# Turning z of the first two tiles and u of the last on TensorE instead of by transposing transfers

## The chip, the cores and the metric

The kernel runs on one core of a Trainium2 chip. The metric is the device time of one execution in microseconds; the median of three runs is used. The profile is of one further execution.

## What is computed

```python
# x: (64, 64, 512) fp32; cond: (64,) int32; w_cond: (200, 64, 64)
# w_up: (1024, 512); w_down: (512, 1024)
def hbitlinear(x, w, bits):
    xq = act_quant(fwht(x), bits)      # per token: scale = 127 / max|x|, round, clip, divide
    wq = weight_quant(w)               # ternary, scale = mean|w|
    return einsum('bsd,fd->bsf', xq, wq)

y = einsum('bct,bcd->bdt', x, w_cond[cond])
h = square(relu(hbitlinear(y, w_up, 8)))
out = x + hbitlinear(h, w_down, 8)
```

fwht is the normalized Walsh-Hadamard transform along the last axis (512 elements for y, 1024 for h).

## The kernel before, in words

The 4096 tokens are worked off in 16 tiles of 256 tokens (t = 0 to 15), each made of two pairs of batch entries (k = 0, 1) with 128 tokens each. For each tile the stages are:

- load_x and gather_w (SP's DMA queue): x and the gathered w_cond blocks, the latter into a block-diagonal w_diag.
- x_outer on POOL (x_first on VectorE for tile 0): the outermost butterfly of the first Hadamard transform.
- project(t, h) on TensorE, h = 0, 1: the projection with w_diag into y_ps[h]. y_split (ACT) copies one half out, and y_outer (VectorE) does a further butterfly into y.
- had_z(t, k) on TensorE: the last 128-wide part of the transform, into one PSUM bank (z_ps; for k = 1 of the tiles under EARLY = 4 it is o_ps).
- z_absmax, z_floor, z_invert on VectorE, and quant_z on ACT: z quantized to fp16 integers in zq, with tokens on partitions.
- turn_z(t): one transposing transfer on ACT's DMA queue, zq to zqT, both halves at once.
- up(t, u) on TensorE, u = 0 to 3, into two PSUM buffers h_ps; relu and square on ACT into g.
- g_outer and g_inner on VectorE and g_last on POOL: three butterflies of the second transform. The last tile has half-width forms of these (g_outer_last, g_inner_last, g_last_last).
- had_u(t, k) on TensorE into u_ps (k = 0 of the last two tiles: the banks of h_ps); u_absmax, u_floor, u_invert on VectorE; quant_u on ACT into uq.
- turn_u(t, k): a transposing transfer, uq to uqT, again on ACT's queue.
- down(t, k) on TensorE: eight accumulating matmuls; the residual on VectorE adds x, and SP stores. Tile 14 goes to the banks of y_ps, tile 15 to o_ps and z_ps.

keep_z, token_units and u_unscale on POOL carry the scales along. At the start both weights are loaded in four parts each, summed (weight_abs on ACT and VectorE, weight_sum on TensorE, weight_scale on VectorE), rounded (weight_round, ACT), turned by TensorE (weight_turn, eight transposes into half of u_ps) and evicted (weight_evac, VectorE). warm(i) is four matmuls on constants, which fill TensorE's idle time at the start.

Every engine has its own order of stages, written out by hand: begin() for the pipeline's filling, a step() that the loop repeats for steps 8 to 15, with a fixed lag for every stage, and finish() for its emptying. Semaphores are all that ties the engines together. An engine that waits holds everything behind it in its order. TensorE's finish() ends with:

```python
at(had_u, 15, 0)
at(had_u, 15, 1)
at(down, 14, 1)
at(down, 14, 0)
at(down, 15, 0)
at(down, 15, 1)
```

Of the kernel before, what the change touches and what calls it, by code (L numbers as in the profile page):

```python
# [61 lines left out]
EARLY = 4  # L62
LAST = TILES - 1
# [3 lines left out]
def ffn_kernel(nc, x, cond, w_cond, w_up, w_down, had, out):  # L67
# [7 lines left out]
    with ctx:  # L75
# [102 lines left out]
        s_zqT = sem("zqT_ready")  # L178
        s_kept = sem("z_kept_ready")
# [82 lines left out]
        def _(sp):  # L262
# [43 lines left out]
            at(gather_w, 0, 0)  # L306
            at(load_x, 1, 0)
            at(load_x, 1, 1)
            at(gather_w, 1, 0)
            at(gather_w, 1, 1)  # L310
            load_w_down(3)
            load_w_down(1)
            at(gather_w, 2, 0)
            at(load_x, 2, 0)
            at(load_x, 2, 1)
            at(gather_w, 2, 1)
            load_w_down(0)
            load_w_down(2)
            at(load_x, 3, 0)
            at(gather_w, 3, 0)  # L320
            at(load_x, 3, 1)
            at(gather_w, 3, 1)
            at(load_x, 4, 0)
            at(load_x, 4, 1)
            at(gather_w, 4, 0)
            at(gather_w, 4, 1)
            at(load_x, 5, 0)
            at(gather_w, 5, 0)
# [5 lines left out]
            at(load_x, 7, 0)  # L334
            at(gather_w, 6, 1)
            at(gather_w, 7, 0)
            at(load_x, 7, 1)
            at(load_x, 8, 0)
            at(store, 0, 0)
            at(gather_w, 7, 1)  # L340
            at(store, 1, 0)
            at(store, 0, 1)
            at(gather_w, 8, 0)
            at(load_x, 8, 1)
            at(gather_w, 8, 1)
            at(load_x, 9, 0)
            at(load_x, 9, 1)
            at(store, 2, 0)
            at(store, 1, 1)
            at(gather_w, 9, 0)  # L350
            at(gather_w, 9, 1)
            at(load_x, 10, 0)
            at(store, 2, 1)
            at(store, 3, 0)
            at(gather_w, 10, 0)
            at(gather_w, 10, 1)
            at(load_x, 10, 1)
            at(load_x, 11, 0)
            at(load_x, 11, 1)
            at(store, 3, 1)  # L360
            at(gather_w, 11, 0)
            at(load_x, 12, 0)
            at(store, 4, 1)
            at(load_x, 12, 1)
            at(load_x, 13, 0)
            at(store, 4, 0)
            at(gather_w, 11, 1)
            at(gather_w, 12, 0)
            at(gather_w, 12, 1)
            hold(1)  # L370
            at(store, 5, 0)
            at(gather_w, 13, 0)
            at(load_x, 13, 1)
            at(store, 5, 1)
            at(load_x, 14, 0)
            at(load_x, 14, 1)
            at(load_x, 15, 0)
            at(store, 6, 0)
            at(gather_w, 13, 1)
            at(store, 7, 0)  # L380
            at(store, 6, 1)
            at(store, 7, 1)
            at(load_x, 15, 1)
            at(gather_w, 14, 0)
            at(gather_w, 14, 1)
            at(store, 8, 1)
            at(store, 8, 0)
            at(gather_w, 15, 0)
# [4 lines left out]
            at(store, 10, 0)  # L393
            at(store, 11, 1)
            at(store, 11, 0)
            at(store, 12, 1)
            at(store, 12, 0)
# [10 lines left out]
        def _(pool):  # L408
# [72 lines left out]
            def begin():  # L481
# [4 lines left out]
                at(x_outer, 2, 0)  # L486
                at(x_outer, 3, 0)
                at(x_outer, 3, 1)
                at(keep_z, 1)
                at(x_outer, 4, 1)  # L490
                at(x_outer, 4, 0)
                at(token_units, 0)
# [9 lines left out]
                at(x_outer, 6, 1)  # L502
                at(x_outer, 6, 0)
                at(u_unscale, 0, 1)
                at(token_units, 1)
                at(keep_z, 4)
                at(g_last, 2, 0)
                at(g_last, 2, 1)
                at(u_unscale, 1, 0)
                at(keep_z, 5)  # L510
                at(u_unscale, 1, 1)
                at(x_outer, 7, 0)
                at(token_units, 2)
                at(x_outer, 7, 1)
                at(g_last, 3, 0)
                at(g_last, 3, 1)
                at(u_unscale, 2, 0)
# [12 lines left out]
            def finish():  # L530
                at(token_units, 11)
                at(keep_z, 14)
                at(g_last, 12, 0)
                at(g_last, 12, 1)
                at(u_unscale, 11, 1)
                at(u_unscale, 11, 0)
# [3 lines left out]
                at(g_last, 13, 1)  # L540
                at(u_unscale, 12, 1)
                at(u_unscale, 12, 0)
# [6 lines left out]
                g_last_last(0, 0)  # L549
                at(u_unscale, 14, 0)  # L550
                g_last_last(1, 0)
                at(u_unscale, 14, 1)
                at(token_units, 15)
                at(u_unscale, 15, 1)
                at(u_unscale, 15, 0)
# [4 lines left out]
        def _(act):  # L560
# [81 lines left out]

            def load_had():
                act.dma_start(had_sb[:, :], had[:, 0, 0:P]).then_inc(s_had, 16)

            def begin():
                load_had()
                load_w_up(1)
                gather_first(0)
                gather_first(1)  # L650
                load_w_up(0)
                load_w_up(2)
                at(y_split, 0, 1)
                at(y_split, 0, 0)
                weight_abs(0, 0)
                load_w_up(3)
                weight_abs(0, 2)
                at(y_split, 1, 1)
                at(quant_z, 0, 0)
                at(y_split, 1, 0)  # L660
                at(quant_z, 0, 1)
                weight_round(0, 0)
                weight_round(0, 1)
                at(turn_z, 0)
                weight_round(0, 2)
                weight_round(0, 3)
                weight_abs(1, 1)
                weight_abs(1, 3)
                at(relu, 0, 1)
                at(relu, 0, 0)  # L670
                at(quant_z, 1, 1)
                at(y_split, 2, 1)
                at(y_split, 2, 0)
                at(square, 0, 0)
                at(quant_z, 1, 0)
                weight_round(1, 0)
                at(y_split, 3, 0)
                weight_round(1, 1)
                at(relu, 0, 2)
                at(turn_z, 1)  # L680
                at(relu, 0, 3)
                at(square, 0, 1)
                at(y_split, 3, 1)
                weight_round(1, 2)
                at(relu, 1, 0)
                at(relu, 1, 1)
                weight_round(1, 3)
                at(quant_z, 2, 0)
                at(y_split, 4, 0)
                at(quant_z, 2, 1)  # L690
                at(relu, 1, 3)
                at(y_split, 4, 1)
                at(relu, 1, 2)
# [3 lines left out]
                at(square, 1, 0)  # L697
                at(relu, 2, 1)
                at(quant_u, 0, 0)
                at(quant_z, 3, 1)  # L700
                at(relu, 2, 0)
                at(relu, 2, 3)
                at(turn_u, 0, 0)
                at(square, 2, 0)
                at(relu, 2, 2)
                at(y_split, 5, 1)
                at(turn_z, 3)
                at(y_split, 5, 0)
                at(quant_z, 4, 0)
                at(quant_u, 0, 1)  # L710
                at(square, 2, 1)
                at(quant_z, 4, 1)
                at(relu, 3, 0)
                at(relu, 3, 1)
                at(turn_z, 4)
                at(y_split, 6, 0)
                at(quant_u, 1, 0)
                at(quant_z, 5, 0)
                at(relu, 3, 3)
                at(turn_u, 0, 1)  # L720
                at(relu, 3, 2)
                at(y_split, 6, 1)
                at(square, 3, 0)
                at(quant_z, 5, 1)
                at(quant_u, 1, 1)
                at(square, 3, 1)
                at(turn_u, 1, 0)
                at(relu, 4, 1)
                at(turn_u, 1, 1)
                at(relu, 4, 0)  # L730
                at(relu, 4, 3)
                at(turn_z, 5)
                at(quant_u, 2, 0)
                at(relu, 4, 2)
                at(quant_z, 6, 0)
                at(y_split, 7, 0)
                at(quant_u, 2, 1)
                at(square, 4, 1)
                at(y_split, 7, 1)
                at(turn_u, 2, 0)  # L740
# [690 lines left out]
```

## Time and profile before

| | |
|---|---|
| median of 3 runs | 264.64 us (263.68 to 269.92) |
| the profiled execution's own time | 267.76 us |
| its span, first to last instruction | 266.0 us |
| TensorE busy | 247.5 us, 93% |
| VectorE busy | 210.4 us, 79% |
| POOL busy | 192.3 us, 72% |
| ACT busy | 146.4 us, 55% |
| TensorE's mean granted clock | 0.992 of full speed |

Busy times are of one execution, and engines work side by side. PE is TensorE, DVE VectorE, ACT ScalarE, POOL GpSimd and SP SyncE; "ACTq" and "SPq" are DMAs as issued by these engines. L879 is a line of the kernel: L837 warm, L847 project, L864 had_z, L827 weight_turn, L879 up, L900 had_u, L917 down on TensorE; L598 quant_z, L634 quant_u, L608 turn_z, L641 turn_u on ACT; L1060 weight_abs, L1092 weight_evac, L1106 y_outer, L1111 z_absmax, L1136 g_inner, L1168 u_absmax, L1187 residual on VectorE; L461 g_last on POOL; L282 gather_w and L292 load_w_down on SP. An fp32 matmul shows up as two passes.

### The profile page before, as it was taken

How to read it: one execution, taken by the hardware profiler on the slowest of the kernel's cores; microseconds unless marked ns; L12 is line 12 of the kernel's file. 1: busy time of each engine (PE TensorE's matmuls, PEld its weight loads, DVE VectorE, ACT ScalarE, POOL GpSimd, SP SyncE). 2: the span in 40 equal slices, each digit the busy share in tenths (PEclk: the TensorE clock that was granted, in tenths of full speed). 3: DMA queues.
4: the chain of work that ended last, by engine and by line, in shares of the span. 5: the costliest groups of instructions: out<-in, count | busy, mean ns of one | idle time of the engine just before them, and what ended most of it. 6: DMA issues, size and time to landing. Idle time of an engine off the chain costs nothing. (4 is left out here: it accounts for less than half of the span.)

```text
span 266.0 us, 6425 instructions
## 1 busy us (share of the span) xinstructions
PE 247.5 (93%) x1932; PEld 205.7 (77%) x1932; DVE 210.4 (79%) x385; ACT 146.4 (55%) x209; POOL 192.3 (72%) x231
## 2 busy tenths in 40 slices
PE   6996979999998999999999999999999999999775
PEld 6985979989878688787878788887888788667531
DVE  0666587988989799697969698897969989779952
ACT  0557677775754647382737457372827575563330
POOL 2123379769496899897989989897979586968420
PEclk9999799999999999999999999999999999999999
DMA  6989480864243955365735582451635425725464
GB/s 182 305 272 249 116 131 8 165 118 136 39 92 113 184 160 136 80 166 140 195 93 121 139 226 39 119 137 36 155 86 118 80 69 92 161 46 151 68 163 166
DMA packets 66856, 34.95 MB, mean 131 GB/s; under 512 B 56978, under 2 KB 57106, under 8 KB 66834
## 3 DMA queue, kind: packets, MB, share of 16 engines
q10 hardware_dynamic: 52080, 14.78, 29.8%
q1 hardware_dynamic: 14754, 19.90, 24.5%
q8 instruction: 10, 0.16, 0.3%
q14 instruction: 12, 0.10, 0.1%
HBM read 13.70 MB, written 8.39 MB: 83 GB/s over the span
## 5 line engine op out<-in xcount | busy, mean ns | idle before, releaser
L461 POOL TENSOR_TENSOR p<-g 128x512 f32<-128x512 f32 x60 | 75.0, 1281 | 15.8 <-DVE g L1136 12.9
L879 PE MATMUL h_ps<-zqT,w_upT 128*128 128x256 f16 x512 | 64.5, 275 | 4.1 <-DMA zqT<-zq 4.1
L900 PE MATMUL u_ps<-had_sb,p 128*128 128x128 f32 x480 | 59.3, 277 | 3.9 <-ACT uq L634 3.0
L900 PEld LDWEIGHTS u_ps<-had_sb,p 128*128 128x128 f32 x480 | 56.6, 192 | 8.1 <-issue 5.7
L634 ACT ACTIVATE uq<-u_ps,u_mul 128x1024 f16<-128x1024 f32 x30 | 33.4, 1114 | 50.1 <-DVE u_mul L1181 50.1
L879 PEld LDWEIGHTS h_ps<-zqT,w_upT 128*128 128x128 f16 x512 | 50.0, 99 | 13.3 <-DMA zqT<-zq 5.0
L917 PE MATMUL o_ps<-w_downT,uqT 128*128 128x512 f16 x232 | 54.8, 379 | 3.4 <-DMA uqT<-uq 2.8
L424 POOL TENSOR_TENSOR x_half<-x_all 128x512 f32 (+1 forms) x30 | 37.6, 1272 | 24.8 <-DMA x_all<-in_x_dram 14.8
L615 ACT ACTIVATE g<-h_ps 128x512 f32<-128x512 f32 x64 | 35.9, 596 | 22.0 <-PE h_ps L879 12.7
L917 PEld LDWEIGHTS o_ps<-w_downT,uqT 128*128 128x128 f16 x232 | 22.4, 98 | 25.3 <-DMA uqT<-uq 4.4
L1168 DVE TENSOR_REDUCE u_max<-u_ps 128x1 f32<-128x1024 f32 x30 | 36.5, 1217 | 4.7 <-PE u_ps L900 4.5
L1130 DVE TENSOR_TENSOR g<-g 128x1024 f32<-128x1024 f32 x30 | 36.7, 1254 | 2.4 <-issue 1.4
L1187 DVE SCALAR_TENSOR_TENSOR out_sb<-o_ps,u_deq,x_all 128x512 f32<-128x512 f32 x29 | 21.7, 749 | 20.4 <-PE o_ps L917 19.8
L1136 DVE TENSOR_TENSOR g<-g 128x1024 f32<-128x1024 f32 x30 | 35.9, 1236 | 0.0
L847 PE MATMUL y_ps<-w_diag,x_half 128*128 128x128 f32 x256 | 34.4, 281 | 1.0 <-issue 0.6
L478 POOL TENSOR_TENSOR u_deq<-u_abs,out_unit 128x1 f32<-128x1 f32 x32 | 21.6, 679 | 16.4 <-DVE out_sb L1187 8.0
L847 PEld LDWEIGHTS y_ps<-w_diag,x_half 128*128 128x128 f32 x256 | 31.8, 197 | 1.8 <-issue 1.5
L623 ACT ACTIVATE g<-g 128x1024 f32<-128x1024 f32 x30 | 31.4, 1054 | 1.4 <-issue 1.0
L864 PE MATMUL z_ps<-had_sb,y 128*128 128x128 f32 x224 | 30.3, 278 | 0.0
L864 PEld LDWEIGHTS z_ps<-had_sb,y 128*128 128x128 f32 x224 | 27.3, 191 | 1.5 <-ACT zq L598 0.5
L1106 DVE TENSOR_TENSOR y<-y_ps,y_odd 128x256 f32<-128x256 f32 x64 | 23.9, 417 | 4.7 <-ACT y_odd L593 4.5
L441 POOL TENSOR_SCALAR up_unit<-z_now,up_scale 128x2 f32<-128x2 f32 x32 | 23.1, 736 | 2.8 <-POOL z_now L436 2.8
(61 smaller groups left out, 214.6 us busy)
## 6 DMA issues: line engine op xcount, KB each, us to landing
x_all<-in_x_dram SPq DMA_DIRECT2D x32, 256.0 KB, 3.4
out_dram<-out_sb SPq DMA_DIRECT2D x32, 256.0 KB, 2.3
w_raw<-in_L_ffn_w_up_dram ACTq DMA_DIRECT2D x4, 512.0 KB, 4.6
w_raw<-in_L_ffn_w_down_dram SPq DMA_DIRECT2D x4, 512.0 KB, 6.1
w_diag<-in_L_cond_weights_dram SPq DMA_DIRECT2D x62, 16.0 KB, 2.4
uqT<-uq ACTq DMA_TRANSPOSE x32, 3.1
zqT<-zq ACTq DMA_TRANSPOSE x16, 3.2
had_sb<-in_hadamard_dram ACTq DMA_DIRECT2D x1, 64.0 KB, 1.9
```

The source lines that it names most:

```text
L424: nc.gpsimd.tensor_tensor(x_half[h][:, :, :], xt[:, :, 0, :], xt[:, :, 1, :], (ALU.add, ALU.subtract)[h]).then_inc(s_xh[h], 1)
L461: nc.gpsimd.tensor_tensor(new[:, :, m, :], old[:, :, 0, :], old[:, :, 1, :], (ALU.add, ALU.subtract)[m]).then_inc(s_p8[k], 1)
L615: nc.scalar.activation(g[par][:, 2 * u:2 * u + 2, :], h_ps[u % 2], ACT.Relu, scale=1.0 / UNIT)\
L634: nc.scalar.activation(uq[k][:, :], u_bank(t, k), ACT.Copy, scale=u_mul[:, k:k + 1])\
L847: mm = nc.tensor.matmul(y_ps[h][:, l, j * P:(j + 1) * P], x_half[h][:, j, l * P:(l + 1) * P], w[:, j, :], start=True, stop=True)
L864: mm = nc.tensor.matmul(z_bank(t, k)[:, c * P:(c + 1) * P], y[par][:, c, k * P:(k + 1) * P], had_sb[:, :], start=True, stop=True)
L879: mm = nc.tensor.matmul(h_all[:, u % 2, i, :], w_upT[:, q, f * P:(f + 1) * P], zqT[par][:, :, q, :], start=(q == 0), stop=(q == TC - 1))
L900: mm = nc.tensor.matmul(u_bank(t, k)[:, c * P:(c + 1) * P], p8[par][:, c, k * P:(k + 1) * P], had_sb[:, :], start=True, stop=True)
L917: mm = nc.tensor.matmul(o_bank(t, k), uqT[par][k][:, m, :], w_downT[:, m, :], start=(m == 0), stop=(m == FC - 1))
L1130: nc.vector.tensor_tensor(g2[:, n, :, :], g[par][:, 0:4, :], g[par][:, 4:8, :], (ALU.add, ALU.subtract)[n]).then_inc(s_g2, 1)
L1136: nc.vector.tensor_tensor(p4[par][:, :, n, :], g2[:, :, 0:2, :].rearrange("p h a n -> p h (a n)"), g2[:, :, 2:4, :].rearrange("p h a n -> ...
L1168: nc.vector.tensor_reduce(u_max[:, k:k + 1], u_bank(t, k), AX.X, ALU.max, apply_absolute_value=True).then_inc(s_umax[k], 1)
```

## The change

z of tiles 0 and 1 (BYPE = 2) and u of tile 15 are no longer turned by a transfer. TensorE transposes them in fp16 against the identity into PSUM banks that are free at that time. z goes back into the bank from which it was quantized, and VectorE copies it to zqT. u of half k goes into two banks, the first half copied by VectorE, the second by ACT. The waits that counted finished z transfers are shifted by two tiles. had_z of tiles 1 and 2 waits for the copies as well. The orders of begin() and finish() are written anew on every engine; step() is unchanged on all of them.

```diff
+BYPE = 2
+        zT_ps = [b[:, :].bitcast(FP16)[:, 0:T] for b in (z_ps, o_ps)]
+        uT_ps = [[b.bitcast(FP16)[:, 0:T] for b in two]
+                 for two in ((h_all[:, 0, :, :].rearrange("p l n -> p (l n)"),
+                              h_all[:, 1, :, :].rearrange("p l n -> p (l n)")),
+                             (u_ps[:, 0:T], u_ps[:, T:2 * T]))]
...
             def quant_z(t, half, par, k):
-                after(act, s_zqT, 16 * (t - 1))
+                if isinstance(t, int) and t < BYPE + 2:
+                    after(act, s_zturn[k], t - 1)
+                else:
+                    act.wait_ge(s_zqT, 16 * (t - 1 - BYPE))
...
+            def uT_evac(k):                                  # ACT
+                act.wait_ge(s_uturn[2 * k + 1], 1)
+                act.wait_ge(s_o[k], LAST - 1)
+                nc.scalar.activation(uqT[LAST % 2][k][:, 4:8, :].rearrange("p m n -> p (m n)"), uT_ps[k][1],
+                                     ACT.Copy).then_inc(s_uT[2 * k + 1], 1)
...
             def had_z(t, half, par, k):
                 if isinstance(t, int) and t <= EARLY:
+                    after(pe, s_zT[k], min(t, BYPE))
...
+            def z_turn(t, k):
+                par = t % 2
+                pe.wait_ge(s_ident, 1)
+                pe.wait_ge(s_zq[k], t + 1)
+                for q in range(TC):
+                    mm = nc.tensor.transpose(zT_ps[k][:, q * P:(q + 1) * P], zq[par][:, k, q * P:(q + 1) * P],
+                                             ident[:, :])
+                mm.then_inc(s_zturn[k], 1)
+            def u_turn(k, b):
+                pe.wait_ge(s_uq[k], TILES)
+                for m in range(4):
+                    mm = nc.tensor.transpose(uT_ps[k][b][:, m * P:(m + 1) * P],
+                                             uq[k][:, (4 * b + m) * P:(4 * b + m + 1) * P], ident[:, :])
+                mm.then_inc(s_uturn[2 * k + b], 1)
             def up(t, half, par, u):
-                pe.wait_ge(s_zqT, 16 * t + 16)
+                if isinstance(t, int) and t < BYPE:
+                    for k in range(KP):
+                        pe.wait_ge(s_zT[k], t + 1)
+                else:
+                    pe.wait_ge(s_zqT, 16 * (t + 1 - BYPE))
...
             def down(t, half, par, k):
-                pe.wait_ge(s_uqT[k], 16 * t + 16)
+                if isinstance(t, int) and t == LAST:
+                    pe.wait_ge(s_uT[2 * k], 1)
+                else:
+                    pe.wait_ge(s_uqT[k], 16 * t + 16)
...
                 for m in range(FC):
+                    if isinstance(t, int) and t == LAST and m == 4:
+                        pe.wait_ge(s_uT[2 * k + 1], 1)
...
+            def zT_evac(t, k):                               # VectorE
+                par = t % 2
+                dve.wait_ge(s_zturn[k], t + 1)
+                nc.vector.tensor_copy(zqT[par][:, k, :, :].rearrange("p q n -> p (q n)"), zT_ps[k])\
+                    .then_inc(s_zT[k], 1)
+            def uT_evac(k):                                  # VectorE
+                dve.wait_ge(s_uturn[2 * k], 1)
+                dve.wait_ge(s_o[k], LAST - 1)
+                nc.vector.tensor_copy(uqT[LAST % 2][k][:, 0:4, :].rearrange("p m n -> p (m n)"), uT_ps[k][0])\
+                    .then_inc(s_uT[2 * k], 1)
```

The new orders, where they touch the steps spoken of below (one line for several stages, in order):

```
SP, begin:      load_x 0; gather_w(0,0); gather_w(1,0); load_x 1; gather_w(1,1); load_w_down 1; load_x(2,0);
                load_w_down 0; gather_w(2,0); load_w_down 2; load_x(2,1); load_w_down 3; load_x 3; gather_w(2,1)
                ... load_x 8; hold(1); store(1,1)
ACT, begin:     y_split 0; weight_abs(0,0); load_w_up 3; weight_abs(0,2); quant_z(0,0); quant_z(0,1);
                y_split(1,0); y_split(1,1); weight_round(0,0), (0,1); weight_abs(1,1); weight_round(0,2), (0,3);
                relu(0,0); quant_z(1,0); weight_abs(1,3); relu(0,1); quant_z(1,1); y_split(2,0); weight_round(1,0)
VectorE, begin: x_first 0, 1; y_outer 0; weight_abs(0,1); z_absmax, z_floor, z_invert (0,0); the same (0,1);
                weight_abs(0,3); zT_evac(0,0); weight_scale 0; y_outer(1,0), (1,1); weight_abs(1,0);
                zT_evac(0,1); weight_evac(0,0), (0,1); z_absmax, z_floor, z_invert 1; weight_evac(0,2);
                weight_abs(1,2); weight_evac(0,3); weight_scale 1; zT_evac(1,0); y_outer 2; weight_evac(1,0);
                zT_evac(1,1); weight_evac(1,1); y_outer 3
TensorE, begin: warm x4; project 0; warm x2; had_z 0; warm; project(1,1); z_turn(0,0); project(1,0);
                weight_sum 0; warm x2; z_turn(0,1); weight_turn(0,0); had_z(1,0); weight_turn(0,1); had_z(1,1);
                up(0,0); weight_turn(0,2); up(0,1); weight_turn(0,3); project(2,0); weight_sum 1; z_turn(1,0);
                project(2,1); up(0,2), (0,3); weight_turn(1,0); z_turn(1,1); weight_turn(1,1); project 3;
                had_z(2,0); weight_turn(1,2); up(1,1), (1,0), (1,3), (1,2)
POOL, begin:    token_units 0 moves ahead of x_outer 4, which stands ahead of g_last(0,0)
TensorE, end:   up(15,0); down(11,1); up(15,1); had_u(13,0); up(15,3), (15,2); down(12,0); had_u(13,1);
                down(12,1); had_u(14,0); down(13,0); had_u(14,1); down(13,1); had_u(15,0); down(14,0);
                had_u(15,1); down(14,1); u_turn(0,0), (0,1), (1,0), (1,1); down 15
VectorE, end:   u_absmax(14,0); g_inner_last(1,0), (0,0); u_floor, u_invert (14,0); residual(13,0);
                u_absmax, u_floor, u_invert (14,1); g_outer_last(1,1), (0,1); g_inner_last(0,1), (1,1);
                g_last_last(1,1), (0,1); residual(13,1); u_absmax, u_floor, u_invert (15,0), (15,1);
                uT_evac 0; residual(14,1), (14,0); uT_evac 1; residual 15
ACT, end:       quant_u(15,0), (15,1); uT_evac 0, 1
POOL, end:      g_last_last(0,0), (1,0); u_unscale 14
```

## Rows read from the trace of the kernel before

**Rows 1.** Busy time of each engine by stretch: start:end, length, busy (instructions)

```profile
core 0: us, PE busy (x) PEld busy (x) DVE busy (x) ACT busy (x) POOL busy (x), PEclk, DMA share, GB/s
0.00:60.00 60.00, 52.85 (x455) 49.15 (x456) 39.78 (x87) 36.72 (x57) 30.58 (x38) 0.97 0.69 172
60.00:200.00 140.00, 137.03 (x1068) 113.42 (x1067) 118.28 (x210) 78.55 (x114) 121.21 (x137) 1.00 0.51 123
200.00:266.00 66.00, 57.65 (x412) 43.17 (x410) 52.37 (x90) 31.18 (x40) 40.47 (x58) 0.99 0.50 112
```

**Rows 2.** TensorE's timeline, head: start, us, instruction, [idle before, releaser]

```profile
14.93 2.02 PE L847 MATMUL y_ps<-w_diag,x_half 128*128 128x128 f32 x16 [0.62 <-issue]
...
25.09 2.74 PE L879 MATMUL h_ps<-zqT,w_upT 128*128 128x256 f16 x16 [2.28 <-DMA zqT<-zq]
...
38.77 2.86 PE L879 MATMUL h_ps<-zqT,w_upT 128*128 128x256 f16 x24 [1.66 <-DMA zqT<-zq]
...
46.86 1.95 PE L900 MATMUL u_ps<-had_sb,p 128*128 128x128 f32 x16
```

**Rows 3.** ACT's timeline, head

```profile
16.38 0.68 ACT L598 ACTIVATE zq<-z_ps,z_col 128x512 f16<-128x512 f32 x1
...
18.05 1.62 ACTq L608 DMA_TRANSPOSE zqT<-zq  x1
...
33.37 1.31 ACTq L608 DMA_TRANSPOSE zqT<-zq  x1
```

**Rows 4.** Transfers: of zqT in the whole span, then of uqT from 215 us on

```profile
DMA to landing us min/median/max: 3.0/3.2/7.0
...
DMA to landing us min/median/max: 3.0/3.1/5.3
```

**Rows 5.** The same columns as in rows 1, where the granted clock is low

```profile
26.00:29.40 3.40, 3.40 (x19) 2.98 (x17) 1.88 (x3) 1.77 (x3) 0.00 (x0) 0.50 0.62 174
```

**Rows 6.** The chain that ended last: start, us, what

```profile
253.96 1.22 DVE u_max L1168
...
255.74 3.24 DMA uqT<-uq
...
259.03 1.90 PE o_ps L917 x8
260.94 1.74 PE z_ps L917 x8
```

**Rows 7.** Groups of instructions: count | busy us, mean ns | idle before

```profile
L827 PE MATMUL u_ps<-ident,w_raw 128*128 128x128 f16 x64 | 4.7, 219 | 0.0
...
L1092 DVE TENSOR_SCALAR w_downT<-u_ps 128x1024 f16<-128x1024 f16 x4 | 2.6, 682 | 0.3 <-PE u_ps L827 0.3
```

**Rows 8.** VectorE's timeline, head

```profile
17.83 0.75 DVE L1106 TENSOR_TENSOR y<-y_ps,y_odd 128x256 f32<-128x256 f32 x2
...
26.70 1.22 DVE L1060 TENSOR_REDUCE w_abs<-w_raw 128x1 f32<-128x1024 f32 x1 [0.90 <-DMA w_raw<-in_L_ffn_w_down_dram]
...
39.40 2.36 DVE L1136 TENSOR_TENSOR g<-g 128x1024 f32<-128x1024 f32 x2
```

**Rows 9.** POOL's timeline, head

```profile
42.54 2.51 POOL L461 TENSOR_TENSOR p<-g 128x512 f32<-128x512 f32 x2
```

**Rows 10.** SP's timeline of issues, head

```profile
7.10 4.27 SPq L282 DMA_DIRECT2D w_diag<-in_L_cond_weights_dram  x4
...
18.71 1.37 SPq L292 DMA_DIRECT2D w_raw<-in_L_ffn_w_down_dram  x2
```

**Rows 11.** TensorE's timeline, tail

```profile
233.36 1.90 PE L917 MATMUL o_ps<-w_downT,uqT 128*128 128x512 f16 x8 [1.13 <-DMA uqT<-uq]
...
251.44 2.05 PE L900 MATMUL u_ps<-had_sb,p 128*128 128x128 f32 x16 [0.79 <-DVE p L1163]
```

**Rows 12.** The columns of rows 1, dense stretch of the tail

```profile
240.00:255.00 15.00, 13.03 (x89) 9.66 (x88) 14.38 (x30) 4.68 (x5) 8.79 (x17) 1.00 0.56 129
```

**Rows 13.** ACT's timeline, tail

```profile
247.83 1.25 ACTq L641 DMA_TRANSPOSE uqT<-uq  x1
...
255.65 1.11 ACT L634 ACTIVATE uq<-u_ps,u_mul 128x1024 f16<-128x1024 f32 x1 [0.45 <-DVE u_mul L1181]
```

More of the change, by code:

```diff
@@ L306, in _ @@
             at(gather_w, 0, 0)
+            at(gather_w, 1, 0)
             at(load_x, 1, 0)
             at(load_x, 1, 1)
-            at(gather_w, 1, 0)
             at(gather_w, 1, 1)
+            load_w_down(1)
+            at(load_x, 2, 0)
+            load_w_down(0)
+            at(gather_w, 2, 0)
+            load_w_down(2)
+            at(load_x, 2, 1)
             load_w_down(3)
[L312 to L315, printed above, removed]
+            at(load_x, 3, 0)
+            at(load_x, 3, 1)
             at(gather_w, 2, 1)
-            load_w_down(0)
-            load_w_down(2)
-            at(load_x, 3, 0)
+            at(load_x, 4, 0)
             at(gather_w, 3, 0)
-            at(load_x, 3, 1)
             at(gather_w, 3, 1)
-            at(load_x, 4, 0)
             at(load_x, 4, 1)
@@ L326, in _ @@
             at(gather_w, 4, 1)
+            at(gather_w, 5, 0)
             at(load_x, 5, 0)
-            at(gather_w, 5, 0)
             at(load_x, 5, 1)
@@ L333, in _ @@
             at(load_x, 6, 1)
-            at(load_x, 7, 0)
             at(gather_w, 6, 1)
             at(gather_w, 7, 0)
+            at(load_x, 7, 0)
             at(load_x, 7, 1)
-            at(load_x, 8, 0)
             at(store, 0, 0)
             at(gather_w, 7, 1)
+            at(gather_w, 8, 0)
+            at(store, 0, 1)
+            at(gather_w, 8, 1)
             at(store, 1, 0)
-            at(store, 0, 1)
-            at(gather_w, 8, 0)
+            at(load_x, 8, 0)
             at(load_x, 8, 1)
-            at(gather_w, 8, 1)
+            hold(1)
@@ L360, in _ @@
             at(store, 3, 1)
             at(gather_w, 11, 0)
+            at(gather_w, 11, 1)
+            at(store, 4, 1)
+            at(load_x, 11, 1)
+            at(store, 4, 0)
+            at(gather_w, 12, 0)
+            at(store, 5, 0)
             at(load_x, 12, 0)
-            at(store, 4, 1)
+            at(store, 5, 1)
             at(load_x, 12, 1)
             at(load_x, 13, 0)
-            at(store, 4, 0)
-            at(gather_w, 11, 1)
-            at(gather_w, 12, 0)
+            at(load_x, 13, 1)
@@ L369, in _ @@
+            at(load_x, 14, 0)
             at(gather_w, 12, 1)
-            hold(1)
-            at(store, 5, 0)
             at(gather_w, 13, 0)
[L373 to L377, printed above, removed]
-            at(store, 6, 0)
[L379 to L383, printed above, removed]
+            at(gather_w, 13, 1)
@@ L384, in _ @@
+            at(store, 6, 1)
+            at(store, 6, 0)
             at(gather_w, 14, 0)
             at(gather_w, 14, 1)
+            at(store, 7, 0)
+            at(store, 7, 1)
+            at(load_x, 14, 1)
+            at(gather_w, 15, 0)
             at(store, 8, 1)
+            at(load_x, 15, 0)
             at(store, 8, 0)
-            at(gather_w, 15, 0)
+            at(load_x, 15, 1)
             at(gather_w, 15, 1)
@@ L501, in begin @@
                 at(g_last, 1, 1)
-                at(x_outer, 6, 1)
                 at(x_outer, 6, 0)
@@ L1047, in finish @@
                 at(had_u, 15, 0)
+                at(down, 14, 0)
                 at(had_u, 15, 1)
                 at(down, 14, 1)
-                at(down, 14, 0)
+                u_turn(0, 0)
+                u_turn(0, 1)
+                u_turn(1, 0)
+                u_turn(1, 1)
                 at(down, 15, 0)
@@ L1232, in begin @@
                 at(g_inner, 0, 1)
-                at(y_outer, 3, 1)
                 at(z_absmax, 2, 1)
```

365 lines of the change are left out of this document (189 added, 176 removed).

## The prediction

> **What bounds the kernel now.** I cut the span into three stretches first: TensorE is the busiest engine in each, but from 60 to 200 us it idles for only 3.0 of 140 us, while it idles for 7.2 us before that and for 8.4 us after it [rows 1]. In the middle TensorE is the bound, and that loop is unchanged. So TensorE work that starts earlier in the head should arrive at the end as a whole, and the tail is judged by itself.
>
> Next comes TensorE's timeline of the head. It waits 2.28 us ahead of 25.09 for z of tile 0 out of the transposing transfer, and 1.66 us ahead of 38.77 for that of tile 1 [rows 2]. ACT issued these transfers at 18.05 and 33.37 [rows 3], so they took 7.0 and 5.4 us, where the median of all is 3.2 [rows 4]. After the first gap the granted clock is 0.50 of full speed (1.2 instead of 2.4 GHz) for 3.4 us [rows 5], in which half the work was done: 1.7 us are missing. Sixteen up matmuls take 2.74 us there and twenty-four later take 2.86 [rows 2].
>
> The tail is read from the chain of waits: the last reduction of u on VectorE, the quantization on ACT, the transfer issued at 255.74, and TensorE at 259.03 with 3.65 us for the last two downs [rows 6]. Nothing is left that could cover this transfer.
>
> **Head, removed and added.** Two z transfers go. In their place come four groups of four TensorE transposes and four VectorE copies. The 64 weight transposes take 4.7 us, 0.073 each [rows 7]; so a group costs 0.3 us and the four groups 1.2 us. A VectorE copy of 128x512 fp16 out of PSUM has no row; the nearest is the 128x1024 eviction at 0.68 us [rows 7]. The bounds are 0.34 (half) and 0.68; I take 0.35, as it is the same engine and direction at half the length. That is 1.4 us of VectorE, at most 2.7, where it idles for 20 of 60 us [rows 1].
>
> The chain for tile 0: quant_z(0,0) starts at 16.38 now [rows 3], queued behind y_split(1,1), which waits for the projection that TensorE starts at 14.93 [rows 2]. In the new order floor, reciprocal and quant_z follow the maximum at once, so z(0,0) is there before 16; z_turn(0,0) stands behind project(1,1) and is done by 16.2. The weight sum comes behind the second projection as now, 0.3 us later for the turn. The second half decides. VectorE is through y_outer(1,0) at 18.6 now [rows 8], with (1,1) done before it; in the new order both pairs (0.75 each) follow the weight scale, so 19.4. Then come weight_abs(1,0) (1.22), zT_evac(0,1), done at about 21.0, and weight_evac(0,0), done at 21.7, while TensorE has had_z(1,1) from 21.0 to 21.9. So up(0,0) starts at about 22.0, not at 25.09.
>
> From there I count TensorE's work up to had_u(0,0), at 46.86 now [rows 2]. The 21.8 us in between hold 1.66 of gap and 1.7 of missing clock, so 18.4 of work. Two weight turns (1.2) now come after the first up, and two turns of z of tile 1 are added (0.6): 20.2, so had_u(0,0) could start at 42.2. Its input is the other test: VectorE ends g_inner(0) at 41.8 [rows 8] and POOL's g_last(0,0) starts only at 42.54, behind token_units(0) [rows 9]. With first ups 3.1 us earlier I put the end of g_inner at 39.5 (2.3 earlier, as VectorE has more queued ahead of it) and g_last, 2.5 us and with token_units out of its way, at 42.0. So 42.2: **4.7 us earlier**. The bounds are 2.3 (VectorE's gain, if nothing behind it closes up) and 4.9 (POOL's input). The transfer of tile 2 stays; if it took the 5.4 us that tile 1's did, up(2) would have some 1.5 us of this to give back, which lies inside the bounds.
>
> **Head, orders and queues.** SP issues gather_w(1,0) before load_x(1). Four gathers take 4.27 us at issue [rows 10], so x of tile 1 is issued 2.1 us later. project(1) needs the gathers of tile 1 too, which are issued no later than now, and these cover the x: nothing, and up to 2.1 us if they don't. load_w_down(0) is issued at about 12.7 and no longer behind 18.71. It must land by 19.4, because behind weight_abs(1,0) zT_evac(0,1) and the weight evictions are queued on VectorE, and up(0,0) waits for these. The pair issued from 18.71 on was read by VectorE up to 26.70 with a wait [rows 8, 10], so under 8 us from issue; that makes 20.7 at worst: a loss of 0 to 1.3 us, taken as nothing. hold(1) on SP now means tile 2's transfer, ahead of store(1,1), which is later anyway.
>
> **Tail.** down(12,0) moves behind up(15,3) and up(15,2) and closes the gap of 1.13 us ahead of 233.36 [rows 11]. What is late next is VectorE, busy for 14.4 of the 15 us from 240 on [rows 12]. So this gives between 0 and 1.1; I take 0.8, since that dense stretch starts only after it.
>
> Then the last tile, in the time of the trace of before. down(14,0) now stands ahead of had_u(15,1). Its transfer is issued at 247.83 now [rows 13] and 0.7 us earlier then, because floor and reciprocal of u(14,0) pass a residual (0.75): 247.1, landing at 250.2 with the median of 3.1 us [rows 4]. It runs until 252.0, so had_u(15,1) begins then and not at 251.44 [rows 11], and ends at 253.8. u_absmax(15,1) (1.2), floor and reciprocal (0.4) and quant_u (1.11) [rows 13] end at 256.5. Two groups of u_turn end at 257.1 and down(15,0) starts; VectorE has copied its first half, and ACT's copy of the second (half of 1.11, so 0.6) is done at 257.2, before the fifth matmul. With 3.65 us for both downs: 260.8, against 262.7 now. **Gain 1.9 us.** Bounds: with a transfer of 5.3 us, as one was [rows 4], had_u(15,1) waits 2.2 us more, which makes -0.3; with had_u(15,1) at 251.44 after all it is 2.5.
>
> **A page against this change.** The trace shows the clock falling once, behind weight turns and a gap, and full after the gap of 1.66 us. The Trainium skill, "TensorE: Matmul & The Clock Gate", Part 4, says that the full clock doesn't engage for transposes as for other matmuls; by it the change adds four more such groups to just this stretch, and four ahead of the last two downs. No row here tells whether the gap or the turns made the clock fall.
>
> **The sum.** 4.7 + 0.8 + 1.9 = 7.4 us against the profiled execution's own 267.76 us: 260.4. That execution is 3.1 us above the median of 264.64. Its transfer of 7.0 us and its clock dip of 1.7 us are natural places for the excess, and what the median execution doesn't lose there the change can't give back. With none of the excess there, the median goes to 264.64 - 7.4 = 257.2; with all of it, to 260.3. I take half, 1.55: **258.8 us**.
>
> **Rivals.** (a) The head is held by its next wait: w_down(0) lands late, VectorE waits for it, TensorE for VectorE; or the profiled run's excess was the whole of the gap. For it speaks that VectorE's chain gains only 2.3 us; against it, that VectorE idles a third of the first 60 us. 2.3 - 1.55 + 0.8 + 1.9 = 3.4 gives 261.2; without the 0.8 and with half of the 1.9, 263.0. (b) The transfer that is left in the tail, uqT(14,0), takes the place of the one removed and holds had_u(15,1): 258.8 + 2.2 = 261.0. Against it, the median of 3.1. (c) Slower: the clock stays at 1.2 GHz wherever turns stand, from z_turn(0,0) at 16 to z_turn(1,1) at 30 and over the last two downs. Some 12 us of work in the head and 3.65 in the tail each take twice as long: 258.8 + 15.7 = 274.5. It costs more than the change gives from 5.8 us of work at the low clock on; 1.7 were seen. For it speaks the one dip; against it, the 24 ups at full pace behind the turns of the second weight and a gap. One dip like the seen one more would give 260.5.
>
> **Chances.** Forecast (256.9 to 260.2) 0.50; (a) 0.27; (b) 0.12; better than the forecast 0.06; (c) 0.05, of which 0.02 end beyond 2%. The range from 255.8 to 262.8 leaves some 0.15 out, nearly all above. Two per cent, about what a measurement of this kernel can tell from no change, is 259.35 downward: four fifths of the forecast, the better case, and 0.06 of (a) and (b), 0.52. Within 2% 0.45; slower 0.03.
>
> **What the profile after would show.** up's first matmul near 22 and no wait for zqT ahead of up(0) and up(1); a granted clock that is full from 25 to 30; weight_abs(1,0) without a wait for w_down; turns of 0.3 us a group and copies near 0.35; had_u(0,0) near 42; the unchanged loop at its old pace; in the tail half a us between quant_u(15,1) and down(15,0). I am wrong if the first up starts after 24, if VectorE instead of the transfer holds TensorE in the first 45 us, or if the clock is low for over 4 us.

## The result, and the profile after

The changed kernel takes 261.66 us (median of 8, 260.98 to 262.56), the kernel before 266.18 us in its 8 runs up to then (263.68 to 274.06). The ratio is 0.9865, with a 95% interval of 0.9826 to 0.9905. Each ratio in this document leaves out the executions that took over 1.5% longer than the fastest of the same kernel; the section on the experiments shows what lengthens those of before. The profiled execution of the change took 261.15 us with a span of 259.0, against 267.76 and 266.0. So it gains 6.6 us against the profiled execution of before, and 3.6 us against its usual ones (1.35% of their median of 265.2). I had forecast 7.4 and 5.8. The 261.66 lie above my forecast case (256.9 to 260.2), where I had put rivals (a) and (b).

Busy time by stretch, with the columns of [rows 1]:

```profile
0.00:60.00 60.00, 57.05 (x513) 54.12 (x514) 45.73 (x98) 39.27 (x61) 30.03 (x46) 1.00 0.57 166
60.00:200.00 140.00, 137.17 (x1072) 113.89 (x1071) 118.96 (x212) 80.06 (x116) 122.49 (x134) 1.00 0.55 127
200.00:259.00 59.00, 53.00 (x384) 38.90 (x381) 47.92 (x83) 28.13 (x35) 34.90 (x53) 1.00 0.43 103
```

The head's idle time fell from 7.2 to 3.0 us, the middle is what it was, and the tail idles for 6.0 instead of 8.4. TensorE's timeline of the head, against [rows 2] (L895 is z_turn, L922 up, L943 had_u, L965 down):

```profile
15.79 0.39 PE L895 MATMUL z_ps<-ident,zq 128*128 128x128 f16 x4
16.02 1.11 PE L867 MATMUL y_ps<-w_diag,x_half 128*128 128x128 f32 x8
...
22.02 1.04 PE L922 MATMUL h_ps<-zqT,w_upT 128*128 128x256 f16 x8
...
41.50 1.95 PE L943 MATMUL u_ps<-had_sb,p 128*128 128x128 f32 x16
43.29 1.13 PE L885 MATMUL z_ps<-had_sb,y 128*128 128x128 f32 x8
45.23 2.86 PE L922 MATMUL h_ps<-zqT,w_upT 128*128 128x256 f16 x24 [0.82 <-DMA zqT<-zq]
```

The first up starts at 22.02, not 25.09, and had_u(0,0) at 41.50, not 46.86: 5.4 us earlier. Both waits for a z transfer are gone; the third transfer, which is left, now makes TensorE wait 0.82 us. The granted clock is full throughout, where it was 0.50 for 3.4 us [rows 5]. VectorE, where [rows 8] showed waits for w_down:

```profile
19.26 1.21 DVE L1116 TENSOR_REDUCE w_abs<-w_raw 128x1 f32<-128x1024 f32 x1
20.39 0.41 DVE L1169 COPY zqT<-o_ps 128x512 f16<-128x512 f16 x1
20.72 1.28 DVE L1148 TENSOR_SCALAR w_upT<-u_ps 128x1024 f16<-128x1024 f16 x2
```

w_down had landed when weight_abs(1,0) came, and the copy takes 0.41 us. The tail of TensorE (against [rows 11]) and its chain (against [rows 6]):

```profile
230.39 1.98 PE L943 MATMUL u_ps<-had_sb,p 128*128 128x128 f32 x16
...
240.69 1.89 PE L965 MATMUL o_ps<-w_downT,uqT 128*128 128x512 f16 x8 [1.18 <-DVE out_sb L1257]
...
246.25 2.05 PE L943 MATMUL u_ps<-had_sb,p 128*128 128x128 f32 x16
248.13 1.89 PE L965 MATMUL y_ps<-w_downT,uqT 128*128 128x512 f16 x8
250.04 0.62 PE L903 MATMUL h_ps<-ident,uq 128*128 128x128 f16 x8
251.61 0.62 PE L903 MATMUL u_ps<-ident,uq 128*128 128x128 f16 x8 [0.95 <-ACT uq L649]
```

```profile
250.44 1.12 ACT uq L649
251.56 0.05 issue
251.61 0.62 PE u_ps L903 x8
252.23 1.73 PE o_ps L965 x8
253.95 1.74 PE z_ps L965 x8
```

From had_u(15,1) to the first matmul of down(15,0) it took 259.03 - 251.44 = 7.59 us and takes 252.06 - 246.25 = 5.81. From had_u(0,0) to had_u(15,1) it took 204.58 and takes 204.75. So the 7.0 us between the two spans are 5.4 in the head, -0.2 up to had_u(15,1) and 1.8 in the last tile.

On the way to had_u(15,1) something is gained and lost again. These are had_u(13,1) on TensorE and g_last_last on VectorE (its last two additions), before and then after; had_u(13,1) after is the line at 230.39 above:

```profile
236.85 1.95 PE L900 MATMUL u_ps<-had_sb,p 128*128 128x128 f32 x16
```

```profile
250.09 1.29 DVE L1163 TENSOR_TENSOR p<-g 128x512 f32<-128x512 f32 x2
```

```profile
244.90 1.29 DVE L1233 TENSOR_TENSOR p<-g 128x512 f32<-128x512 f32 x2
```

From had_u(0,0) to had_u(13,1) it took 189.99 us and takes 188.89, 1.1 less. From had_u(0,0) to g_last_last it took 203.23 and takes 203.40.

### The profile page after: what moved, and what is told of

Read it like the earlier page. It is cut to its first block and busy times, and to the rows that moved or that the text cites. A ratio compares the mean times of both kernels' runs of the same rounds, so it can differ in the third digit from the quotient of the medians.

```text
span 259.0 us, 6500 instructions
## 1 busy us (share of the span) xinstructions
PE 247.2 (95%) x1964; PEld 206.9 (80%) x1964; DVE 212.6 (82%) x391; ACT 147.5 (57%) x211; POOL 187.4 (72%) x231
## 5 line engine op out<-in xcount | busy, mean ns | idle before, releaser
L922 PE MATMUL h_ps<-zqT,w_upT 128*128 128x256 f16 x512 | 63.7, 273 | 0.9 <-DMA zqT<-zq 0.8
L943 PEld LDWEIGHTS u_ps<-had_sb,p 128*128 128x128 f32 x480 | 56.7, 192 | 6.8 <-issue 4.4
L943 PE MATMUL u_ps<-had_sb,p 128*128 128x128 f32 x480 | 59.2, 277 | 2.3 <-ACT uq L649 2.1
L922 PEld LDWEIGHTS h_ps<-zqT,w_upT 128*128 128x128 f16 x512 | 49.5, 98 | 10.1 <-DMA zqT<-zq 1.3
L965 PE MATMUL o_ps<-w_downT,uqT 128*128 128x512 f16 x232 | 54.8, 379 | 1.2 <-DVE out_sb L1257 1.2
L965 PEld LDWEIGHTS o_ps<-w_downT,uqT 128*128 128x128 f16 x232 | 22.6, 98 | 22.3 <-issue 1.3
L490 POOL TENSOR_TENSOR u_deq<-u_abs,out_unit 128x1 f32<-128x1 f32 x32 | 25.4, 797 | 15.3 <-DVE out_sb L1257 8.3
L867 PE MATMUL y_ps<-w_diag,x_half 128*128 128x128 f32 x256 | 33.5, 276 | 1.0 <-POOL x_half L436 1.0
L867 PEld LDWEIGHTS y_ps<-w_diag,x_half 128*128 128x128 f32 x256 | 30.8, 192 | 1.2 <-issue 1.2
L613 ACT ACTIVATE zq<-z_ps,z_col 128x512 f16<-128x512 f32 x28 | 19.1, 684 | 13.5 <-DVE z_col L1193 10.1
```

The source lines that it names most:

```text
L867: mm = nc.tensor.matmul(y_ps[h][:, l, j * P:(j + 1) * P], x_half[h][:, j, l * P:(l + 1) * P], w[:, j, :], start=True, stop=True)
L922: mm = nc.tensor.matmul(h_all[:, u % 2, i, :], w_upT[:, q, f * P:(f + 1) * P], zqT[par][:, :, q, :], start=(q == 0), stop=(q == TC - 1))
L943: mm = nc.tensor.matmul(u_bank(t, k)[:, c * P:(c + 1) * P], p8[par][:, c, k * P:(k + 1) * P], had_sb[:, :], start=True, stop=True)
L965: mm = nc.tensor.matmul(o_bank(t, k), uqT[par][k][:, m, :], w_downT[:, m, :], start=(m == 0), stop=(m == FC - 1))
```

## The experiments

The theory after this reading: the kernel before is held in its head by the time at which its first transfer lands; that differs from execution to execution, and the profiled one was a bad one, so the usual execution has much less to gain there (theory 1 below). The rival: the head gives its 4.7 us to every execution, and the measured 3.6 is what something later takes back.

**The kernel before, again,** without an edit, twelve executions:

> The kernel before, unchanged, for the clock and span of many executions. Theory 1 (the excess of the profiled execution lies in the head): executions near 265 us have a mean granted clock of 0.998 or more, no low clock around 26 to 29 us, a first transfer that lands under 6 us from issue, and had_u(0,0) at 43.5 to 45 instead of 46.86. Theory 2 (it lies in the middle or is around the span): had_u(0,0) stays at 46.5 to 47 in an execution of 265 us, and the loop's period or the distance from span to time is shorter instead.

Median 264.56 us (262.81 to 271.5), 0.9976 [0.9931, 1.0021] of before. The three with a clock under 0.995 took 266.9 to 271.5. The profiled one took 266.25 (span 264.5). It had had_u(0,0) at 44.61, where theory 1 put it. But its first transfer took 7.3 us, not under 6. Its clock stayed full behind a gap as long as the one of before, so the gap doesn't always bring the low clock:

```profile
25.08 1.92 PE L879 MATMUL h_ps<-zqT,w_upT 128*128 128x256 f16 x16 [2.40 <-DMA zqT<-zq]
...
44.61 1.95 PE L900 MATMUL u_ps<-had_sb,p 128*128 128x128 f32 x16
```

**The kernel before, three single executions,** to find what one near 263.5 us does:

> The kernel before, one execution. Theory 1 (executions differ by when the first transfer lands, and the rest follows): had_u(0,0) starts at the span less 219 to 220 us, whatever the span is; for a span near 261.7 that is 42 to 43, with the first transfer landing by 23. Rival (they differ after the head): had_u(0,0) at 44.5 or later for a span under 262.5.

> The kernel before, a second execution: as for the first look.

> The kernel before, a third execution: as for the first look.

They took 264.12, 268.36 and 263.39 us, with spans of 262.3, 266.6 and 261.6. TensorE's timeline of each, in this order:

```profile
23.80 1.92 PE L879 MATMUL h_ps<-zqT,w_upT 128*128 128x256 f16 x16 [0.77 <-DMA zqT<-zq]
42.41 1.95 PE L900 MATMUL u_ps<-had_sb,p 128*128 128x128 f32 x16
```

```profile
25.30 3.60 PE L879 MATMUL h_ps<-zqT,w_upT 128*128 128x256 f16 x16 [2.61 <-DMA zqT<-zq]
...
47.34 1.95 PE L900 MATMUL u_ps<-had_sb,p 128*128 128x128 f32 x16
```

```profile
22.63 1.92 PE L879 MATMUL h_ps<-zqT,w_upT 128*128 128x256 f16 x16
...
42.37 1.95 PE L900 MATMUL u_ps<-had_sb,p 128*128 128x128 f32 x16
```

In the third the first up starts without any wait for the transfer, which took 4.6 us. In the first the transfer took 5.5 us, in the second 7.4: up waits 2.61 us for it and then runs at half the clock. The span less the start of had_u(0,0) is 219.9, 219.3 and 219.2 us here, 219.1 and 219.9 in the two profiles above. So executions differ by 5 us ahead of had_u(0,0) and by 0.8 behind it, as theory 1 has it. An execution that neither a late transfer nor a low clock has lengthened, which I call undisturbed, has had_u(0,0) at 42.4. The change moves that by 0.9 us, not by 5.4. The 0.9 is itself uncertain: the nine profiles with the begin() of the change have had_u(0,0) at 41.16 to 42.39. And the transfer isn't the only wait there: in the first execution up starts 1.2 us later than in the third, and had_u(0,0) stands at 42.4 in both.

**The head alone.** begin() of the change on all engines, finish() of before, u of tile 15 by transfers:

```diff
-                uT_evac(0)                       # ACT, finish(); u_turn and VectorE's copies are out too
-                uT_evac(1)
+                at(turn_u, 15, 0)
+                at(turn_u, 15, 1)
```

> The change's begin() orders and z of tiles 0 and 1 turned by TensorE, with the finish() orders of before and u of tile 15 turned by transfers. Theory 1 (against undisturbed executions of before the head gives about 2 us and the tail 1.6): 263.0 to 263.6 us, 1.6 to 2.0 above the changed kernel. Rival (the head gives nothing in undisturbed executions, all 3.6 us are the tail's): 265.2. In both, had_u(0,0) stands at 41.5 in the profile.

262.60 us (262.14 to 264.11, 12 runs), ratio 0.9960 [0.9931, 0.9990]. had_u(0,0) stood at 42.02. The time is 0.4 us under what theory 1 said, but undisturbed executions of before are quicker here too (a median of 263.65, not 265.2). Against them the head gains 0.4%, 1.1 us, where theory 1 said 2 and the rival 0. All twelve clocks are 0.998 or more, and the long executions of before don't occur: that is the larger part of its worth.

**The tail alone.** `BYPE = 0`, begin() of before, finish() of the change.

> The change's finish() orders and u of tile 15 turned by TensorE, with the begin() orders of before and all z by transfers. Theory 1: 263.3 to 263.9 us in undisturbed executions (1.6 less than 265.2), and the same slow executions near 268 as the kernel before has, since they come from its head. Rival (all 3.6 us are the tail's): 261.6.

261.47 to 263.01 us in four executions, 267 to 269.9 in three: 0.9889 [0.9814, 0.9965] from the four. One half of theory 1 holds: the long executions are still there. The other isn't settled: the median of the four is 262.2, 1.5 us under the 263.65 of before, as theory 1 said (1.6), but the ratio makes 2.9 us of it, with an interval from 0.9 to 4.9 that holds the rival's 3.6 as well. The profiled one, of 269.85 us, shows what a long one has. Its first transfer, issued at 18.27, landed 10.5 us later:

```profile
28.79 3.59 PE L924 MATMUL h_ps<-zqT,w_upT 128*128 128x256 f16 x16 [5.77 <-DMA zqT<-zq]
```

**The gap filled.** The kernel before with eight matmuls on constants behind the first weight's turns:

```diff
                 weight_turn(0, 3)
+                fill(2)
```

> The kernel before with eight matmuls on constants (1.8 us) between the last turn of the first weight and up(0,1), where TensorE waits for the first transfer. Theory A (the idle time makes the clock fall): the low clock around 26 to 29 us is gone, executions of 268 and more become rare, and the median falls by 1 to 1.5 us; undisturbed ones stay at 264 to 265.5. Theory B (the turns of the first weight make it fall): the low clock stays, and the median stays at 266 or rises by up to 1.8.

264.76 us (263.31 to 267.32), ratio 1.0021 [0.9987, 1.0054]. All twelve clocks are 0.999 or more. Without the filling 3 of 12 were under 0.995, and 10 of the 29 executions of before that were timed beside this series. So it is idle time that makes the clock fall, not the turns, which are all still there. The median didn't fall as expected: an execution whose transfer is in time pays for the filling (its fastest is 263.31, against 262.50; in its profile had_u(0,0) stands at 42.98, against 42.4).

**Whether the loads make the first transfer late.** The kernel before, with SP holding 1 MB of w_down, which it issues 0.7 us behind the transfer, until the transfer has landed:

```diff
+            hold(1)
             load_w_down(0)
             load_w_down(2)
```

> The kernel before with SP holding load_w_down(0) and (2) (1 MB, issued 0.7 us behind the first transfer) until that transfer has landed. Theory 1 (the first transfer is slow because its pieces share the DMA engines with loads that are issued around it): it lands within 3.2 to 5 us in every execution, TensorE's wait for it is gone, the granted clock is 0.998 or more in all executions and none is over 267; but w_down is summed later, so the median stays at 263 to 265. Rival (its time varies by itself, or by what was issued before it): still 7 us and more in some executions, clocks under 0.995 among them.

267.69 us (265.55 to 268.46, 6 runs), 1.0118 [1.0069, 1.0168]. In the profiled execution the transfer, issued at 17.74, took 3.9 us and was no longer waited for at 22.33. My expectation of the clock and of the time was wrong: the weight sum now waits for w_down, TensorE idles for 3.36 us, and the clock falls there (0.66 from 30 to 35 us). It falls once more in the tail, behind a wait of 1.96 us for a transfer of u (0.50 from 249 to 251 us).

```profile
22.33 1.91 PE L880 MATMUL h_ps<-zqT,w_upT 128*128 128x256 f16 x16
...
29.38 0.35 PE L818 MATMUL u_ps<-w_abs,ones 128*128 128x4 f32 x2 [3.36 <-issue]
```

**z by transfers in the new orders.** `BYPE = 0`; z_turn and zT_evac left out, turn_z(0) and turn_z(1) put behind quant_z(0,1) and quant_z(1,1) on ACT. Here all of w_down and four pairs of x are issued from 11 to 18.7 us, around the transfer's issue at 15.88.

> The changed kernel with z of tiles 0 and 1 turned by transfers again (new orders kept, the TensorE turns and VectorE copies of z left out). Theory 1 (what counts is when the first transfer lands, and it often lands in time): the quickest executions within 0.5 us of the changed kernel's 261 to 261.6, others 2 to 7 us above it, some with a granted clock under 0.995; median 262 to 264. Rival (turning on TensorE gives a fixed gain in every execution): no execution under 263.5.

270.66 us (266.14 to 272.04, 6 runs), 1.0136 [1.0059, 1.0213] from two of them. Theory 1 is wrong here: it had the quickest within 0.5 us of the changed kernel. The rival's number holds, none under 263.5, but its reason, a fixed gain, is not what the profile shows. There the transfer landed 13.5 us after its issue:

```profile
15.88 1.37 ACTq L623 DMA_TRANSPOSE zqT<-zq  x1
```

```profile
29.38 1.89 PE L924 MATMUL h_ps<-zqT,w_upT 128*128 128x256 f16 x8 [7.25 <-DMA zqT<-zq]
```

So the first transfer took 3.9 us with half of w_down held back, 13.5 with all of w_down around it, and 3.8, 4.6, 5.5, 7.0, 7.3, 7.4 and 10.5 in the seven profiles in which that half is issued up to 1.6 us behind it. That the loads make it late fits this, but isn't shown: each of the two outer cases is one profile, and the 3.8 us (before_filled) came without any holding. Why it differs so much between executions with the same loads stays open. What is shown is that the new order of loads, with this transfer in it, takes 266 us and more, and without it 261.

**u by transfers in the new orders.** turn_u(15,0) and (15,1) again, without u_turn and its copies.

> The changed kernel with u of tile 15 turned by two transfers again, all orders else kept. Theory 1 (the turn is the tail's whole gain, the finish() orders give nothing net): 1.7 to 1.9 us above the changed kernel, 263.0 to 263.6, as narrow a band as its own. Rival (the finish() orders are the gain): within 0.5 us of it.

265.31 us (264.35 to 267.52), 1.0048 [1.0016, 1.0080]: 4.0 us above the changed kernel on the same chip (261.27), twice what theory 1 said, where the rival said next to nothing. The clock was 0.985 to 0.994 in every execution. The last downs waited 3.72 us, and ran at half the clock, the second one behind a transfer of 5.5 us:

```profile
253.39 3.59 PE L960 MATMUL o_ps<-w_downT,uqT 128*128 128x512 f16 x8 [3.72 <-DMA uqT<-uq]
257.16 3.00 PE L960 MATMUL z_ps<-w_downT,uqT 128*128 128x512 f16 x8 [0.18 <-DMA uqT<-uq]
```

To tell the two causes apart, twelve matmuls on constants were put in front of down(15,0):

```diff
                 at(down, 14, 1)
+                warm(16)
+                warm(17)
+                warm(18)
```

> The changed kernel with u of tile 15 turned by transfers, and twelve matmuls on constants (2.7 us) between down(14,1) and down(15,0), where TensorE otherwise waits 3.7 us. Theory 1 (of the 4.0 us that the transfers cost in these orders, 1.8 are the transfer's latency and the rest the low clock that the idle time brings): clock 0.998 or more, 263.0 to 263.6. Rival (the transfers themselves take longer in these orders): the clock is full, but the time stays over 264.5.

265.39 us (264.81 to 266.88). The clock is 0.999 or more in eight of the twelve executions, the profiled one among them, and the time is no better (the eight took 264.81 to 265.98), so it is the transfers. Counted from had_u(15,1), down(15,0) starts after 7.50 us and down(15,1) after 11.37, where the changed kernel has 5.81 and 7.54:

```profile
252.11 5.65 DMA uqT<-uq
257.76 0.05 issue
257.81 1.92 PE z_ps L960 x8
```

In the order of before the last transfer took 3.24 us [rows 6], and down(15,1) started 9.33 us behind had_u(15,1). Here tile 14's residuals are stored at the same time; that this is why it takes 5.65 is an argument, and no run shows it.

**The turn in the old order of the tail.** head_only with u_turn, the first half between the two downs of tile 14:

```diff
                 at(had_u, 15, 1)
                 at(down, 14, 1)
+                u_turn(0, 0)
+                u_turn(0, 1)
                 at(down, 14, 0)
+                u_turn(1, 0)
+                u_turn(1, 1)
```

> The change with the finish() orders of before, in which both downs of tile 14 stand behind had_u(15,1); u of tile 15 turned by TensorE, the first half between those two downs. Theory 1 (the turn can give its 1.8 us only where had_u(15,1) and down(15,0) aren't kept apart by the downs of tile 14): 0.7 to 1.0 us under the 262.6 of the same kernel with transfers, so 261.6 to 261.9, 0.3 to 0.6 above the changed kernel. Rival (the new finish() orders cost in VectorE's dense stretch what they give): 260.8 to 261.2, as fast as the changed kernel or faster.

261.94 us (260.79 to 263.31), 0.9922 [0.9890, 0.9953]: 0.7 less than the 262.60 of the head alone, as theory 1 said, though the two intervals overlap at their ends; down(15,0) starts 6.68 us behind had_u(15,1) (head_only 7.60, the changed kernel 5.81).

**down(14,0) back** behind down(14,1) in the changed kernel, so that both stand between had_u(15,1) and the turns:

> The changed kernel with down(14,0) back behind down(14,1), so both stand between had_u(15,1) and the turns of u. Theory 1 (its 1.73 us of TensorE then lie on the path, and the idle time before had_u(15,1) is lost): down(15,0) starts about 0.9 us later after had_u(15,1) than in the changed kernel (6.7 instead of 5.8), so 262.1 to 262.5. Rival (VectorE's chain to the last quantization is all that counts): the same time as the changed kernel within 0.3.

Five of twelve executions took 261.84 to 262.22, as expected; the other seven, six of them with a clock of 0.992 or 0.993, took 263.3 to 265.0; median 263.58, 0.9958 [0.9919, 0.9998]. In the profiled one TensorE waits 1.89 us for VectorE ahead of had_u(15,1), and the clock falls behind this wait (0.50 from 248 to 250 us). So down(14,0) ahead of had_u(15,1) does two things: it leaves the stretch between had_u(15,1) and down(15,0), where the first group of five loses the 0.9 us that theory 1 gave it, and it keeps TensorE at work.

```profile
246.27 2.64 PE L943 MATMUL u_ps<-had_sb,p 128*128 128x128 f32 x16 [1.89 <-DVE p L1233]
248.70 4.74 PE L965 MATMUL y_ps<-w_downT,uqT 128*128 128x512 f16 x16
```

**down(12,0) back** ahead of up(15,3) and up(15,2):

> The changed kernel with down(12,0) back ahead of up(15,3) and up(15,2). By my prediction it loses 0.8 us: 262.1. By the reading of the two traces (1.05 us gained ahead of had_u(13,1), all of it lost again before g_last_last ends) it loses 0 to 0.3 us: 261.3 to 261.6, as long as its transfer lands within 4 us.

262.19 us (261.32 to 263.39), 0.9943 [0.9914, 0.9972]; had_u(15,1) comes 205.31 us behind had_u(0,0), in the changed kernel 204.75 and, in its second profile, 204.73. By these distances the step is worth 0.6 us, by the medians 0.9 (from runs on two chips): nearer to my prediction than to my reading of the traces. The six other profiles with the new begin() and finish() have 204.70 to 204.96 us there, so the step stands clear of their spread.

**residual(13,0) first,** ahead of u_floor(14,0) as in the kernel before:

> The changed kernel with residual(13,0) back ahead of u_floor(14,0) on VectorE. Theory 1 (the 1.05 us that moving down(12,0) gave were lost in VectorE's dense stretch, 0.7 of them where u_floor(14,0) waits for kappa of POOL with nothing ahead of it): 0.6 to 0.8 us less than the changed kernel. Rival (kappa, or the squares, hold the last tile anyway): no difference within 0.2, with the idle time at another place of the same stretch.

261.72 us (260.80 to 263.23), 0.9898 [0.9863, 0.9933], no difference from the changed kernel. The rival holds. The idle time is gone from VectorE, but its next pair takes 0.7 us longer, as POOL's g_last_last (240.54 to 243.03) now runs beside it for 0.9 us; in the changed kernel the two meet for 0.2 us. The changed kernel first, then this one:

```profile
242.03 1.36 DVE L1216 TENSOR_TENSOR g<-g 128x512 f32<-128x512 f32 x2
```

```profile
242.11 2.06 DVE L1216 TENSOR_TENSOR g<-g 128x512 f32<-128x512 f32 x2
```

**The changed kernel again:**

> The changed kernel, unchanged, beside the part kernels on one chip. Both theories: a narrow band, 260.8 to 262.6 us, granted clock 0.998 or more in every execution, since no transfer stands ahead of the first ups. If the head gives only what the first transfer loses in a given execution, undisturbed executions of before (near 263.3) are 1.5 to 2.5 us slower than it, nearly all of it the tail's; if the head gives 4.7 us as predicted against every execution, none of before's may lie under 266.

261.27 us (260.84 to 263.19, 6 runs), 0.9897 [0.9854, 0.9940]; clocks 0.998 to 1. Before took 263.26 to 268.52 beside it, so the head doesn't give 4.7 us against every execution. No version tried has a median under that of the changed kernel.

## Why the prediction was right, and where it was wrong

- **The head against the profiled execution: right, and a little small.** up(0,0) at 22.0 (22.02), had_u(0,0) at 42.2 (41.50), 4.7 us (5.4). The count of TensorE's work was right to 0.7 us, and w_down was in time. The copies take 0.41, not 0.35, the groups of turns 0.23 from start to start, not 0.3.
- **"I take half" of the profiled execution's excess: the step that failed.** The 3.1 us that the profiled execution stood above the median were head time as a whole, and more: an undisturbed execution has had_u(0,0) at 42.4, 4.5 us before the profiled one. I took 1.55 us off the head's 4.7 and left 3.15; what an undisturbed execution gains there is 0.9. My upper end, "with all of it, to 260.3", was too low as well, because I bounded what the median execution doesn't lose by the distance of two times, where the profile had shown the stalls themselves: 2.28 of gap and 1.7 of missing clock, behind a transfer that took 7.0 us where its median was 3.2. The 0.9 are 42.4 - 41.5; with -0.2 up to had_u(15,1) and 1.8 in the last tile the sum is 2.5 us. The second series of the changed kernel has 1.0% or 2.7 us, the first 3.6; the 1.1 us between the sum and the first stay unexplained. In the first the usual executions of before, five of them, had a median of 265.2; in two later series they had 263.65 and 264.27. So I forecast 258.8 and a gain of over 2%, and the gain is 1.0 to 1.4%.
- **Tail orders, 0.8 us: about right as a part, gone in the sum, the second term that failed.** Moving down(12,0) brings had_u(13,1) 1.1 us closer to had_u(0,0) and is worth some 0.6 by itself. But from had_u(0,0) to had_u(15,1) nothing is gained: 204.75 us, where five profiles of the kernel before have 204.58 to 205.39, and two with the new begin() and the old finish() 204.33 and 204.51. The dense stretch of VectorE takes it back: u_absmax(13,1) starts 6.43 us before its old time and g_last_last ends 5.2 before. My bound of 0 was the one to take for the sum.
- **The last tile, 1.9 us: right (1.8).** Its parts are shown too, by the distance from had_u(15,1) to down(15,0): 7.60 us, 6.68 with the transposes alone, 5.81 with down(14,0) moved as well, so 0.9 each.
- **The page against this change.** Four more groups of turns in the head and four in the tail leave the clock full: 0.998 to 1 in all 14 executions. Filling the idle time, with all turns in place, removed the low clock in the kernel before. Rival (c) has nothing left for it, and the rule of the Trainium skill ("TensorE: Matmul & The Clock Gate", Part 4) changed nothing here, with matmuls around every group.
- **Rival (a)** gave 261.2, which is near, and its second branch, in words, is what happened (the excess was the whole of the gap). But the number is luck: it was added up from a head gain of 2.3 us, half of the excess and 0.8 of tail orders, and the runs show none of the three. Its first branch, w_down late, didn't happen. **Rival (b)** didn't happen: down(14,0) started at 244.20, well before had_u(15,1).

## What to carry to other kernels

When one profiled execution stands above the median of the times, look for the stall in it that can vary, and take the gain from it as gone for the usual execution before anything else. Here that was a transfer issued among large loads, which took from 3.8 to 13.5 us. Taking it off the path narrowed the times (260.8 to 263.2 instead of 262.5 to 274.1) by more than it lowered the best of them, and the order of loads that suits the kernel without the transfer was far worse with it.

## What the runs showed of the hardware

- TensorE's clock fell to half in or behind idle times of 1.89, 1.96, 2.28, 2.61, 3.36, 3.72, 5.77 and 7.25 us; it stayed full behind 1.63, 1.66, 1.97 and 2.40 us. So the length of one idle time didn't decide it alone.
- The same transposing transfer of z of tile 0 took 3.8, 3.9, 4.6, 5.5, 7.0, 7.3, 7.4, 10.5 and 13.5 us in nine profiles.
- Two VectorE additions of 128x512 took 1.36 us with 0.2 us of them beside POOL's additions, and 2.06 us with 0.9 us beside them.
